# A decoder layer on one core: where the softmax work of its last stage runs

## Chip, cores and metric

One Trainium2 chip, one of its cores. The metric is the device time of one execution in microseconds (us). The arithmetic is float32; in the last stage the projections of the attention are done with float32 values split in two parts.

## What is computed

A layer on x of 32 sequences x 64 tokens x 512: a selective-scan block, a cross-attention to ctx_4096 (also 32 x 64 x 512) and a mixture of 64 rank-8 experts, each behind a layer norm and added to x. The change touches the cross-attention alone:

```python
q = (query @ Wq).reshape(nb, q_len, H, D).transpose(0, 2, 1, 3)      # H = 32 heads, D = 128
k = (key @ Wk).reshape(nb, q_len, KVH, D).transpose(0, 2, 1, 3)      # KVH = 8
v = (value @ Wv).reshape(nb, q_len, KVH, D).transpose(0, 2, 1, 3)
q = q * cos + _rotate_half(q) * sin
k = k * cos + _rotate_half(k) * sin
k = jnp.repeat(k, GROUPS, axis=1)                                    # GROUPS = 4
v = jnp.repeat(v, GROUPS, axis=1)
scores = jnp.einsum('bhqd,bhkd->bhqk', q, k) / jnp.sqrt(jnp.float32(D))
scores = jnp.where(mask == 0, jnp.float32(-1000000000.0), scores)
attn = jax.nn.softmax(scores, axis=-1)
x = jnp.einsum('bhqk,bhkd->bhqd', attn, v)
return x.transpose(0, 2, 1, 3).reshape(nb, q_len, H * D) @ Wo
```

## The kernel before

The 2048 tokens are four blocks of 512 (8 sequences each). Every engine runs one hand-written program, `one(i, mamba, attn, nxt)`, five times: stage 0 does the scan block of block 0, stages 1 to 3 the scan block of block i beside the attention of block i-1, and the last stage (`mamba` false) only the attention and the experts of the last block. The order on each engine is that of the text; semaphores (`stage` objects, one count per index) tie the engines together.

The attention goes by pairs of heads, o = 0 to 15, in steps: `step(jj, p, tail)` is step o = 2 jj + p. "Even" is p = 0, "odd" p = 1. In the last stage step o has these parts:

- TensorE (PE): `turn_probs` (L1647) transposes the probabilities of o, and waits for them (`prdy`) and for the low part of o-1 (`olo`); `project_o(o-1)` (L1675, 24 matmuls) waits for `olo`; `scores(o+1)` (L1636) waits for the rotated q (`qrdy`) and k (`krdy`); `values(o)` (L1662); `project_q(o+2)` (L1598, 24 matmuls) waits until the scores of o+1 are read (`srd`).
- VectorE (DVE): `mask_scores` (L1227) and `max_scores` (L1233) of o+1; in even steps `rope_k(jj+1)` (L1182, L1183, L1186 with kT and kr); `invert_sum` (L1237) and `probs` (L1241) of o+1; `o_low(o)` (L1287, two instructions: output minus its rounded high part); `rope_q(o+2)` (L1182, L1183, L1186 with qp and qr), which waits for the swapped q (`qrd`).
- ScalarE (ACT): `evac_pt(o)` (L879), `exps(o+1)` (L865: 8 instructions of 64 columns, each with its maximum as bias and its sum accumulated), `evac_o(o)` (L888), `swap_q(o+2)` (L839, L840).
- GpSimd (POOL): `split_wq(o+2)` and `split_wo(o+1)`: for each a TENSOR_SCALAR for the high part (L673) and a TENSOR_TENSOR for the low part (L675), of 128x1024 floats in SBUF. `split_wo(o+1)` waits for `project_o(o-1)` and is followed by the q split of the next step.
- SyncE (SP) loads the weights; before it loads the next k it waits for `krdy`, with later weight loads behind it.

Steps 0 to 12 that are even rotate a k, seven in all; steps 14 and 15 (`tail`) have no q to project, and step 15 no softmax. `rope_k` reads k1, kr, cosT and sinT, all in SBUF; `rope_q` reads PSUM and cosT (L1182), qr and sinT (L1183), qp and qr (L1186).

Of the kernel before, what the change touches and what calls it, by code (L numbers as in the profile page):

```python
# [25 lines left out]
P = 128  # L26
# [53 lines left out]
def build(nc, a, out):  # L80
    ctx = ExitStack()
    with ctx:
# [152 lines left out]
        def stage(name, per):  # L235
            return Stage(nc, ctx, name, per)
# [102 lines left out]
        wos = stage("wo_split", PAIRS)  # L339
        olo = stage("o_lo_ready", PAIRS)  # L340

        x2r = stage("x2_ready", TT)
# [462 lines left out]
        def _(eng):  # L805
# [26 lines left out]
            def one(i, mamba, attn, nxt):  # L832
# [28 lines left out]
                def exps(jj, o):  # L861

                    eng.wait_ge(smx.sem, smx.upto(blk, o) + jj * 2)
                    for b in range(NB):
                        ins = S.activation(pr[:, b, :], sc[:, b, :], ACT.Exp, bias=mx[:, b:b + 1],  # L865
                                           accum_out=sm[:, b:b + 1])
                    ins.then_inc(exd.sem, 1)
# [37 lines left out]
                def step(jj, p, tail):  # L905
# [6 lines left out]
                    if mamba:  # L912
                        decay(jj, p, 2)
                        decay(jj, p, 3)
                    if attn and not last:
                        exps(jj, p + 1)
                    if mamba and not last:
                        decay(jj, p + 1, 0)
                    if attn:
                        evac_o(jj, p)  # L920
# [157 lines left out]
        def _(eng):  # L1078
            lead(eng, ln1, ln1n, cv, ssv, ssi, sstr, spd, ur, inr, ch_n, ch_c, ch_f, scd, hcd, yad, pid, qt1, qt2, kt1, kt2, qrdy,
                 krdy, q1r, q2r, srd, smx, rcp, prdy, x2r, ln3, ln3n, rmd, zgd, outr, ch_p, ch_a, yr, x1r,  # L1080
                 ln2, ln2n, ch_m, olo)
            V = nc.vector
# [90 lines left out]
            def times_c(i, jj, p, c):  # L1173

                eng.wait_ge(scd.sem, scd.upto(i, NCH * p + c) + jj * (2 * NCH))
                h3 = hs[:, c, :].rearrange("p (d t) -> p d t", t=T)
                V.tensor_tensor(h3, h3, bc[:, p, 1:2, :].to_broadcast([P, 2, T]), ALU.mult).then_inc(hcd.sem, 1)  # L1177

            def attention_of(blk, mamba):
# [50 lines left out]
                def max_scores(jj, o):  # L1230

                    eng.wait_ge(srd.sem, srd.upto(blk, o) + jj * 2)
                    V.tensor_reduce(mx[:, :], sc[:, :, :], AX.X, ALU.max, negate=True).then_inc(smx.sem, 1)  # L1233

                def invert_sum(jj, o):
                    eng.wait_ge(exd.sem, exd.upto(blk, o) + jj * 2)
                    V.reciprocal(sm[:, :], sm[:, :]).then_inc(rcp.sem, 1)  # L1237
# [5 lines left out]

                return rope_q, rope_k, mask_scores, max_scores, invert_sum, probs

# [3 lines left out]
            def one(i, mamba, attn, nxt):  # L1249
                blk = i - 1  # L1250
                rope_q, rope_k, mask_scores, max_scores, invert_sum, probs = attention_of(blk, mamba)
                if not mamba:
# [14 lines left out]
                if attn:  # L1267
                    eng.wait_ge(s_mask, blk * 32 + 32)
                    eng.wait_ge(rop.sem, rop.upto(blk, 0))
                    rope_k(0)  # L1270
                    rope_q(0, 0)
                    for part in (mask_scores, max_scores, invert_sum, probs):
                        part(0, 0)
                    rope_q(0, 1)
# [17 lines left out]
                def step(jj, p, tail):  # L1292
# [15 lines left out]
                    if soft:  # L1308
                        max_scores(jj, p + 1)
                    if not mamba and not tail and p == 0:  # L1310
                        rope_k(jj + 1)
                    if mamba:
# [4 lines left out]
                    if mamba:  # L1317
                        times_c(i, jj, p, 2)
                    if soft:
                        invert_sum(jj, p + 1)  # L1320
                    if mamba:
                        times_c(i, jj, p, 3)
                    if soft and not mamba:
                        probs(jj, p + 1)
                    if not mamba:
                        o_low(jj, p)
                    if attn and not tail:
# [719 lines left out]
```

## Time and profile before

| | us |
|---|---|
| median of 3 runs | 2364.16 (2362.36 to 2365.87) |
| the profiled execution | 2367.41 |
| its span in the trace | 2365.6 |
| PE busy | 2095.8 (89%) |
| DVE busy | 1802.3 (76%) |
| ACT busy | 1058.3 (45%) |
| POOL busy | 588.8 (25%) |

The chain that ended last is, over the whole span, 41% DVE, 31% PE, 16% issue, 6% DMA and 4% ACT. The last stage is a small part of the span, so these shares say little of it; it is read by its own window, its own part of the chain and the timeline of its steps. In a timeline each line is a start, a duration, the engine, the line of the program, the operation with output and inputs, and in brackets how long the engine had been idle and what released it.

### The profile page before, as it was taken

Reading aid. Unit: us, or ns where it says so; the run is one execution under the profiler, and the core shown is the slowest. Engines: PE = TensorE matmul, PEld = TensorE weight load, DVE = VectorE, ACT = ScalarE, POOL = GpSimd, SP = SyncE. Lnnn points to the kernel's source line nnn. Section 1 sums busy time; section 2 is a strip of 40 time slices with the busy share of each in tenths; the row PEclk is TensorE's granted clock in tenths of the full one; section 3 lists DMA queues with packets and bytes.
Section 4 is the critical chain, followed back from the end, with each engine's and each line's share of the span. In section 5 each row is a group of like instructions: output and inputs, shape, how many; then the busy total and the mean of one; then the engine's idle time right before and its main releaser. Section 6 shows DMA issues by size and latency. Waiting matters only on the chain.

```text
span 2365.6 us, 27225 instructions
## 1 busy us (share of the span) xinstructions
PE 2095.8 (89%) x8272; PEld 1188.3 (50%) x8272; DVE 1802.3 (76%) x1816; ACT 1058.3 (45%) x2615; POOL 588.8 (25%) x408
## 2 busy tenths in 40 slices
PE   6877888989999979998999988998999979799988
PEld 2332453445555534445555543445555544477774
DVE  3499994389999985259999996359999995355653
ACT  2544441465555522266555542255655550243331
POOL 0089991001111111001111111001111111556650
PEclk9788999889999999989999999989999999899999
DMA  1468984238888881237888873236888874322310
GB/s 63 157 159 195 213 211 132 63 125 178 172 192 177 177 193 45 84 114 154 176 176 193 178 151 105 80 111 135 176 184 167 186 148 132 112 89 85 98 58 18
DMA packets 110121, 328.98 MB, mean 139 GB/s; under 512 B 12992, under 2 KB 13120, under 8 KB 107616
## 3 DMA queue, kind: packets, MB, share of 16 engines
q0 software_dynamic: 35328, 127.94, 29.1%
q1 hardware_dynamic: 68960, 189.58, 26.7%
q10 hardware_dynamic: 5760, 10.49, 1.2%
q8 instruction: 45, 0.74, 0.1%
q14 instruction: 28, 0.23, 0.0%
HBM read 183.00 MB, written 14.94 MB: 84 GB/s over the span
## 4 chain that ended last, share of the span: by engine, by line
DVE 41%; PE 31%; issue 16%; DMA 6%; ACT 4%; DVEq 1%; SPq 1%; POOL 1%; POOLq 0%; ACTq 0%; PEldq 0%
DVE hs L1170 13%; PE acc L1553 5%; DVE hs L1177 5%; DMA xc<-hs 4%; DVE hs L1342 4%; PE acc L1675 4%; DVE hs L1161 3%; PE pq L1606 2%; DVE qr L1207 2%; PE acc L1688 2%; PE acc L1767 2%; PE pq L1844 2%; PE pq L1636 2%; DVE sc L1227 2%; PE pk L1844 2%
## 5 line engine op out<-in xcount | busy, mean ns | idle before, releaser
L713 POOL DMA_DIRECT2D xc<-hs x192 | 165.8, 866 | 1305.9 <-DVE hs L1177 1269.0
L1170 DVE TENSOR_TENSOR_SCAN hs<-dA,hs 128x1024 f32<-128x1024 f32 x192 | 429.0, 2277 | 0.0
L900 ACT ACTIVATE dA<-dt,aneg 128x504 f32<-128x504 f32 x384 | 253.5, 707 | 253.6 <-DVE hs L1170 253.4
L1606 PE MATMUL pq<-qT,wa 128*128 128x512 f32 x768 | 353.8, 615 | 9.4 <-DVE sc L1227 9.4
L1688 PE MATMUL acc<-wb,oT 128*128 128x512 f32 x768 | 354.9, 607 | 3.6 <-ACT oT L888 3.6
L1177 DVE TENSOR_TENSOR hs<-hs,bc 128x1024 f32<-128x1024 f32 x256 | 308.2, 1206 | 2.2
L865 ACT ACTIVATE pr<-sc,mx 128x64 f32<-128x64 f32 x512 | 170.8, 335 | 243.1 <-DVE mx L1233 243.1
L1553 PE MATMUL acc<-xnT,wa 128*128 128x512 f32 x512 | 232.3, 607 | 12.4 <-PE acc L1553 4.7
L1606 PEld LDWEIGHTS pq<-qT,wa 128*128 128x128 f32 x768 | 146.6, 196 | 183.3 <-issue 173.1
L1161 DVE TENSOR_TENSOR hs<-u,bc 128x1024 f32<-128x1024 f32 x192 | 226.5, 1220 | 11.2 <-ACT xc L983 5.9
L1688 PEld LDWEIGHTS acc<-wb,oT 128*128 128x128 f32 x768 | 142.4, 195 | 149.7 <-issue 145.6
L1636 PE MATMUL pq<-kT,qp 128*128 128x64 f32 x1024 | 187.4, 285 | 23.8 <-DVE qp L1186 14.0
L1636 PEld LDWEIGHTS pq<-kT,qp 128*128 128x128 f32 x1024 | 158.0, 202 | 56.4 <-issue 40.6
L1553 PEld LDWEIGHTS acc<-xnT,wa 128*128 128x128 f32 x512 | 96.4, 193 | 146.5 <-issue 130.5
L1638 PE MATMUL pq<-k2T,qr 128*128 128x64 f32 x768 | 154.4, 284 | 0.0
L1227 DVE COPY_PREDICATED sc<-mask,pq 128x512 f32<-128x512 int32 x64 | 46.6, 729 | 104.2 <-PE pq L1636 58.6
L1638 PEld LDWEIGHTS pq<-k2T,qr 128*128 128x128 f32 x768 | 122.4, 201 | 0.0
L738 POOL TENSOR_TENSOR qp<-u,bc 128x1024 f32<-128x1024 f32 x32 | 92.9, 2904 | 107.9 <-ACT xc L983 107.7
L1647 PE MATMUL pk<-ident,pr 128*128 128x128 f32 x256 | 43.0, 294 | 83.8 <-ACT pr L873 62.0
L738 POOL TENSOR_TENSOR qr<-u,bc 128x1024 f32<-128x1024 f32 x32 | 100.5, 3141 | 7.2 <-DVE hs L1342 7.2
L1119 DVE SCALAR_TENSOR_TENSOR xc<-acc,cw,xc 128x504 f32<-128x504 f32 (+2 forms) x96 | 69.9, 734 | 42.1 <-ACT xc L823 39.6
L1620 PEld LDWEIGHTS pk<-wv,ctxT 128*128 128x128 f32 x768 | 87.7, 192 | 25.5 <-issue 24.5
(234 smaller groups left out, 3363.5 us busy)
## 6 DMA issues: line engine op xcount, KB each, us to landing
xc<-hs POOLq DMA_DIRECT2D x240, 512.0 KB, 7.0
bc<-bc_rows SPq DMA_DIRECT2D x64, 512.0 KB, 7.5
wa<-in_wq SPq DMA_DIRECT2D x64, 512.0 KB, 9.8
wb<-in_wo SPq DMA_DIRECT2D x64, 512.0 KB, 5.2
wa<-in_wx SPq DMA_DIRECT2D x16, 512.0 KB, 4.6
wa<-in_wz SPq DMA_DIRECT2D x16, 512.0 KB, 6.1
wb<-in_ow SPq DMA_DIRECT2D x16, 512.0 KB, 6.3
k<-k_rows SPq DMA_DIRECT2D x32, 256.0 KB, 11.1
```

What stands on the lines that cost most here:

```text
L713: G.dma_start(xc[:, 2 * c:2 * c + 2, :], hs[:, c, :].rearrange("p (d t) -> p d t", t=T), accum_op=ALU.add).then_inc(s_y[c], 16)
L738: G.tensor_tensor(inputs[c % 2].rearrange("p (d t) -> p d t", t=T), u[:, 2 * c:2 * c + 2, :], bc[:, p, 0:1, :].to_broadcast([P, 2, T]), AL ...
L865: ins = S.activation(pr[:, b, :], sc[:, b, :], ACT.Exp, bias=mx[:, b:b + 1], accum_out=sm[:, b:b + 1])
L900: ins = S.activation(to[:, :, 1:SEQ], dt[:, s, :].rearrange("p (b t) -> p b t", t=SEQ)[:, :, 1:SEQ], ACT.Exp, scale=aneg[:, s, bass.ds(jj ...
L1161: V.tensor_tensor(hs[:, c, :].rearrange("p (d t) -> p d t", t=T), u[:, 2 * c:2 * c + 2, :], bc[:, p, 0:1, :].to_broadcast([P, 2, T]), ALU. ...
L1170: V.tensor_tensor_scan(out=hs[:, c, :], data0=dA[:, c % 2, :], data1=hs[:, c, :], initial=0.0, op0=ALU.mult, op1=ALU.add).then_inc(scd.sem, 1)
L1177: V.tensor_tensor(h3, h3, bc[:, p, 1:2, :].to_broadcast([P, 2, T]), ALU.mult).then_inc(hcd.sem, 1)
L1553: ins = M.matmul(banks(s % 4), wa4((s // 2) % 2)[:, k, (s % 2) * P:(s % 2 + 1) * P], xnT[:, k, :], start=(k == 0), stop=(k == KE - 1))
L1606: ins = M.matmul(pq[:, h, :], wa4(p)[:, k, h * P:(h + 1) * P], qT[:, k, :], start=(k == 0), stop=(k == KE - 1))
L1636: ins = M.matmul(pq[:, 0, seq], qp[:, b, :], kT[:, seq], start=True, stop=not mamba)
L1638: ins = M.matmul(pq[:, 0, seq], q2[:, b, :], k2T[:, seq], start=False, stop=True)
L1688: ins = M.matmul(acc[:, t, :], oT[:, h, t * P:(t + 1) * P], wb2(o % 2)[:, h, :], start=False, stop=(stop and h == 1))
```

## The change

In the last stage only (`not mamba`):

- `max_scores` signals a semaphore of its own; a new `shift_scores` on VectorE adds the (negated) maxima to the scores, writing them to pr; one exponential on ScalarE works on all 512 columns of pr in place; a new `sum_probs` on VectorE adds up the probabilities, and `invert_sum` waits for it. The 8 exponentials with bias and accumulated sum are gone there.
- ScalarE evacuates the output (`evac_o`) ahead of the exponential of the next pair, not behind it.
- VectorE makes the low part of o between `shift_scores` and `sum_probs`, not behind `probs`.
- `rope_k(jj+1)` moves from behind `max_scores` to behind `probs`, ahead of `rope_q`.

```diff
--- before.py
+++ after.py
@@ -338,6 +338,8 @@
         woh = stage("wo_hi", PAIRS)
         wos = stage("wo_split", PAIRS)
         olo = stage("o_lo_ready", PAIRS)
+        lmx = stage("last_scores_max", PAIRS)
+        psm = stage("last_probs_summed", PAIRS)
 
         x2r = stage("x2_ready", TT)
         ln3 = stage("ln3_variance", 1)
@@ -861,6 +863,9 @@
                 def exps(jj, o):
 
                     eng.wait_ge(smx.sem, smx.upto(blk, o) + jj * 2)
+                    if not mamba:
+                        S.activation(pr[:, :, :], pr[:, :, :], ACT.Exp).then_inc(exd.sem, 1)
+                        return
                     for b in range(NB):
                         ins = S.activation(pr[:, b, :], sc[:, b, :], ACT.Exp, bias=mx[:, b:b + 1],
                                            accum_out=sm[:, b:b + 1])
@@ -912,11 +917,13 @@
                     if mamba:
                         decay(jj, p, 2)
                         decay(jj, p, 3)
+                    if not mamba:
+                        evac_o(jj, p)
                     if attn and not last:
                         exps(jj, p + 1)
                     if mamba and not last:
                         decay(jj, p + 1, 0)
-                    if attn:
+                    if mamba and attn:
                         evac_o(jj, p)
                     if mamba and not last:
                         decay(jj, p + 1, 1)
@@ -1078,7 +1085,7 @@
         def _(eng):
             lead(eng, ln1, ln1n, cv, ssv, ssi, sstr, spd, ur, inr, ch_n, ch_c, ch_f, scd, hcd, yad, pid, qt1, qt2, kt1, kt2, qrdy,
                  krdy, q1r, q2r, srd, smx, rcp, prdy, x2r, ln3, ln3n, rmd, zgd, outr, ch_p, ch_a, yr, x1r,
-                 ln2, ln2n, ch_m, olo)
+                 ln2, ln2n, ch_m, olo, lmx, psm)
             V = nc.vector
             eng.wait_ge(s_init, 3)
             eng.wait_ge(s_aneg, 1)
@@ -1230,10 +1237,25 @@
                 def max_scores(jj, o):
 
                     eng.wait_ge(srd.sem, srd.upto(blk, o) + jj * 2)
-                    V.tensor_reduce(mx[:, :], sc[:, :, :], AX.X, ALU.max, negate=True).then_inc(smx.sem, 1)
+                    V.tensor_reduce(mx[:, :], sc[:, :, :], AX.X, ALU.max, negate=True).then_inc(
+                        smx.sem if mamba else lmx.sem, 1)
+
+                def shift_scores(jj, o):
+
+                    eng.wait_ge(lmx.sem, lmx.upto(0, o) + jj * 2)
+                    V.tensor_tensor(pr[:, :, :], sc[:, :, :], mx[:, :].unsqueeze(2).to_broadcast([P, NB, SEQ]),
+                                    ALU.add).then_inc(smx.sem, 1)
+
+                def sum_probs(jj, o):
+
+                    eng.wait_ge(exd.sem, exd.upto(blk, o) + jj * 2)
+                    V.tensor_reduce(sm[:, :], pr[:, :, :], AX.X, ALU.add).then_inc(psm.sem, 1)
 
                 def invert_sum(jj, o):
-                    eng.wait_ge(exd.sem, exd.upto(blk, o) + jj * 2)
+                    if mamba:
+                        eng.wait_ge(exd.sem, exd.upto(blk, o) + jj * 2)
+                    else:
+                        eng.wait_ge(psm.sem, psm.upto(0, o) + jj * 2)
                     V.reciprocal(sm[:, :], sm[:, :]).then_inc(rcp.sem, 1)
 
                 def probs(jj, o):
@@ -1241,14 +1263,15 @@
                     V.tensor_tensor(pr[:, :, :], pr[:, :, :], sm[:, :].unsqueeze(2).to_broadcast([P, NB, SEQ]),
                                     ALU.mult).then_inc(prdy.sem, 1)
 
-                return rope_q, rope_k, mask_scores, max_scores, invert_sum, probs
+                return rope_q, rope_k, mask_scores, max_scores, shift_scores, sum_probs, invert_sum, probs
 
             norm_in(0)
             convolve(0)
 
             def one(i, mamba, attn, nxt):
                 blk = i - 1
-                rope_q, rope_k, mask_scores, max_scores, invert_sum, probs = attention_of(blk, mamba)
+                rope_q, rope_k, mask_scores, max_scores, shift_scores, sum_probs, invert_sum, probs = attention_of(
+                    blk, mamba)
                 if not mamba:
 
                     for k in range(KE):
@@ -1269,8 +1292,13 @@
                     eng.wait_ge(rop.sem, rop.upto(blk, 0))
                     rope_k(0)
                     rope_q(0, 0)
-                    for part in (mask_scores, max_scores, invert_sum, probs):
-                        part(0, 0)
+                    mask_scores(0, 0)
+                    max_scores(0, 0)
+                    if not mamba:
+                        shift_scores(0, 0)
+                        sum_probs(0, 0)
+                    invert_sum(0, 0)
+                    probs(0, 0)
                     rope_q(0, 1)
                 if mamba:
                     softplus(i, ch)
@@ -1307,8 +1335,6 @@
                         times_c(i, jj, p, 1)
                     if soft:
                         max_scores(jj, p + 1)
-                    if not mamba and not tail and p == 0:
-                        rope_k(jj + 1)
                     if mamba:
                         scan_input(i, jj, p, 2)
                         scan_input(i, jj, p, 3)
@@ -1316,14 +1342,20 @@
                         scan(i, jj, p, 3)
                     if mamba:
                         times_c(i, jj, p, 2)
+                    if soft and not mamba:
+                        shift_scores(jj, p + 1)
+                    if not mamba:
+                        o_low(jj, p)
+                    if soft and not mamba:
+                        sum_probs(jj, p + 1)
                     if soft:
                         invert_sum(jj, p + 1)
                     if mamba:
                         times_c(i, jj, p, 3)
                     if soft and not mamba:
                         probs(jj, p + 1)
-                    if not mamba:
-                        o_low(jj, p)
+                    if not mamba and not tail and p == 0:
+                        rope_k(jj + 1)
                     if attn and not tail:
                         rope_q(jj, p + 2)
                         if mamba and p == 0:
```

## Rows read from the trace of the kernel before

**Rows 1.** Windows of the last stage's steps: busy (instructions), granted clock, DMA share, GB/s.

```profile
2029.00:2303.70 274.70, 237.38 (x1302) 197.16 (x1301) 155.04 (x170) 103.55 (x340) 162.44 (x62) 0.93 0.28 91
```

**Rows 2.** The chain in order of time, last stage: start, us, engine and line.

```profile
2132.81 1.75 PE pq L1636 x16
...
2143.87 5.47 PE acc L1675 x24
2149.34 1.75 PE pq L1636 x16
...
2164.48 1.75 PE pq L1636 x16
...
2175.54 7.07 PE acc L1675 x24
...
2293.97 1.75 PE pq L1636 x16
```

**Rows 3.** Timeline, PE: the transposes of an even step, then of an odd one.

```profile
2143.24 0.63 PE L1647 MATMUL pk<-ident,pr 128*128 128x128 f32 x4 [1.93 <-DVE oT_lo L1287]
...
2158.39 0.63 PE L1647 MATMUL pk<-ident,pr 128*128 128x128 f32 x4 [0.57 <-DVE oT_lo L1287]
```

**Rows 4.** Timeline, DVE: even step 4.

```profile
2134.78 0.74 DVE L1227 COPY_PREDICATED sc<-mask,pq 128x512 f32<-128x512 int32 x1 [2.76 <-PE pq L1636]
2135.55 0.69 DVE L1233 TENSOR_REDUCE mx<-sc 128x8 f32<-128x512 f32 x1
2136.16 2.65 DVE L1182 TENSOR_TENSOR kT<-k,cosT 128x512 f32<-128x512 f32 x1
2138.73 1.52 DVE L1183 TENSOR_TENSOR kr<-kr,sinT 128x512 f32<-128x512 f32 x1
2140.36 0.69 DVE L1186 TENSOR_TENSOR kT<-kT,kr 128x512 f32<-128x512 f32 x1
...
2141.20 0.69 DVE L1241 TENSOR_TENSOR pr<-pr,sm 128x512 f32<-128x512 f32 x1
...
2143.50 1.22 DVE L1182 TENSOR_TENSOR qp<-pq,cosT 128x1024 f32<-128x1024 f32 x1 [0.41 <-ACT qr L840]
...
2145.96 1.23 DVE L1186 TENSOR_TENSOR qp<-qp,qr 128x1024 f32<-128x1024 f32 x1
```

**Rows 5.** Timeline, POOL: the same step.

```profile
2133.01 2.77 POOL L673 TENSOR_SCALAR wo_hi<-wb 128x1024 fp32r<-128x1024 f32 x1 [3.97 <-PE acc L1675]
2135.86 2.40 POOL L675 TENSOR_TENSOR wo_lo<-wb,wo_hi 128x1024 fp32r<-128x1024 f32 x1
2138.62 2.82 POOL L673 TENSOR_SCALAR wq_hi<-wa 128x1024 fp32r<-128x1024 f32 x1 [0.37 <-POOL wo_lo L675]
2141.52 2.59 POOL L675 TENSOR_TENSOR wq_lo<-wa,wq_hi 128x1024 fp32r<-128x1024 f32 x1
```

**Rows 6.** Timeline, DVE and POOL: the normalisation of odd step 5.

```profile
2155.78 1.26 DVE L1241 TENSOR_TENSOR pr<-pr,sm 128x512 f32<-128x512 f32 x1
...
2155.46 2.77 POOL L673 TENSOR_SCALAR wq_hi<-wa 128x1024 fp32r<-128x1024 f32 x1 [0.68 <-POOL wo_lo L675]
```

**Rows 7.** Timeline, ACT: the end of the swap in step 4.

```profile
2142.45 1.01 ACT L840 ACTIVATE qr<-pq 64x1024 f32<-64x1024 f32 x1
```

**Rows 8.** Groups by line and shape, ACT, whole span: an activation of 512 columns in SBUF.

```profile
L827 ACT ACTIVATE xc<-xc 128x512 f32<-128x512 f32 x32 | 19.9, 622 | 14.7 <-DVE xc L1119 14.6
```

**Rows 9.** Timeline, DVE and POOL: the first q rotation of the stage.

```profile
2042.75 1.87 DVE L1186 TENSOR_TENSOR qp<-qp,qr 128x1024 f32<-128x1024 f32 x1
...
2042.09 3.18 POOL L673 TENSOR_SCALAR wq_hi<-wa 128x1024 fp32r<-128x1024 f32 x1 [0.53 <-POOL wo_lo L675]
```

**Rows 10.** Window of a slow output projection, PE: busy, granted clock, DMA share, GB/s.

```profile
2175.50:2182.60 7.10, 7.10 (x27) 0.76 0.50 164
```

**Rows 11.** Timeline, POOL and PE: the tail's step 14.

```profile
2297.01 2.34 POOL L675 TENSOR_TENSOR wo_lo<-wb,wo_hi 128x1024 fp32r<-128x1024 f32 x1
...
2302.59 1.08 PE L1647 MATMUL pk<-ident,pr 128*128 128x128 f32 x4 [5.79 <-DVE oT_lo L1287]
```

## The prediction

> **What bounds the kernel now.** I read the windows by stage first. The steps of the last stage take 274.70 us, with TensorE busy for 237.38, VectorE for 155.04, ScalarE 103.55 and GpSimd 162.44 [rows 1]. TensorE is near its bound, and a change on other engines can give back at most its idle time. Next the chain in order of time: it repeats by pairs of steps. Call X the end of an output projection, where the next scores begin. From X of step 4 (2132.81) to that of step 5 (2149.34) it is 16.53, and from there to step 6 (2164.48) 15.14 [rows 2]. So an even step costs 1.4 more. The timeline of TensorE says where: ahead of the transposes of the probabilities it idles 1.93 in the even step and 0.57 in the odd one, each time until the low part of o is ready [rows 3]. That low part stands last in VectorE's queue. In the even step the rotation of k stands ahead of it, and there its first multiplication takes 2.65 and its second 1.52, where the subtraction of the same size takes 0.69 [rows 4].
>
> **Who stretches them.** Beside these rows I lay GpSimd's. The multiplication of 2.65 starts at 2136.16 and ends at 2138.81, and GpSimd's subtraction for the weight split runs from 2135.86 to 2138.26 [rows 4, 5]. If the multiplication really works for its usual 0.69, it began at 2138.12, which is 2.26 after GpSimd started. The second starts beside the next split's TENSOR_SCALAR (2138.62) and ends at 2140.25. So it began 0.9 to 1.0 after that, and 2140.36 runs at 0.69 inside the same TENSOR_SCALAR [rows 4, 5]. The normalisation of the odd step, 1.26 for 0.69, ends 1.58 after a TENSOR_SCALAR begins: again 0.9 of waiting [rows 6]. The other way round GpSimd takes 2.59, not 2.40, where the normalisation was running when it came [rows 4, 5]. The reduction at 2135.55 and the masking (one operand from PSUM) keep their usual times [rows 4]. From this I take two prices. A VectorE operation with two operands in SBUF waits until 2.26 behind the start of a GpSimd TENSOR_TENSOR, and 0.9 behind that of a TENSOR_SCALAR. Operations with one operand in SBUF wait for neither.
>
> The Trainium skill (SBUF — State Buffer, section "SBUF: two separate sides") calls this an exclusive lock of a shared port pair, which whichever starts first has "for the whole instruction". The trace agrees for the TENSOR_TENSOR. For the TENSOR_SCALAR it doesn't: the whole 2.8 would have pushed 2140.36 behind 2141.44.
>
> **The even step after, part by part**, in us from X of step 4, if GpSimd keeps its times (low parts at +3.05 and +8.71, high part of q at +5.81) [rows 5]:
> - Mask and maximum end at +3.43 [rows 4]. The added shift is due at +3.46. It reads scores and maxima, both in SBUF, as the normalisation reads its two, and falls into the GpSimd subtraction that stretched the k multiplication. Bounds: 0.69 (nothing holds it, end +4.15) and 2.5 (end +6.00, just where that multiplication ends). I take +6.00, for the slot and the operand places are the same.
> - One exponential for 16 instructions: 0.62 for 512 columns in SBUF is the nearest row [rows 8]; double is a safe upper bound. It starts at +6.04 and ends by +6.7, at worst +7.3. The low part of o (1.28 for both, one operand in PSUM) runs beside it to +7.21, as ScalarE now has o ready by about +4. So the exponential costs nothing; without that cover it would cost its 0.7.
> - The sum of the probabilities is as large as the maximum's reduction, 0.69: end +7.83. It holds up the reciprocal, the normalisation and both rotations behind it, and through them TensorE. Reciprocal (0.20) to +8.06, normalisation to +8.78, clear of the held stretches.
> - Transposes at +8.93, where they now start at 10.43 (2143.24) [rows 3]. TensorE itself is done with the q projection at +8.50 (2143.24 less its idle 1.93). The output projection ends 6.10 behind the transposes (2143.24 to 2149.34 [rows 2, 3]), at +15.03. By this alone the even step would gain 1.5.
> - The moved rotation of k now stands ahead of the rotation of q. It is due at +8.70, and GpSimd's next subtraction at +8.71. Whichever comes first, one of the two multiplications waits out that subtraction. If it is the first, they end at 10.97 + 0.69 + 0.61, and the k subtraction ends at +13.07; if it is the second, +12.95. Unheld it would be +10.8. The swapped q is there at 2143.46, +10.65 [rows 7], so the held rotation delays the q rotation by 2.3.
> - The q rotation takes 3.69 in all (2143.50 to 2147.19) [rows 4]. Its last part, a subtraction with both operands in SBUF, would be due at +15.34 to +15.46. But GpSimd's next split starts 0.20 behind X (2133.01) [rows 5], now at +15.23, and its TENSOR_SCALAR holds that subtraction for 0.9, as one was held in the first q rotation (1.87 for 1.23 [rows 9]). It ends at +17.35, and the scores start at +17.40, against 16.53. TensorE waits 2.37 there.
>
> So the even step loses 0.87 on balance: the gap ahead of the transposes moves to a larger one ahead of the scores.
>
> **The odd step after it.** Its scores start 2.37 late beside GpSimd, so the shift (due +3.46 from the scores) finds the subtraction over. Shift to +4.15, low part to +5.35, sum to +5.96, normalisation to about +6.9. TensorE is busy until about 8.5, so the gap of 0.57 is gone and the step takes 14.5: it gains 0.63.
>
> **SyncE.** The load of the next k waits for the rotated k, now some 5 us later, and two weight loads with it. Each of those tiles is split more than 15 us after it lands now, and the k is read a pair of steps later, so I put this at nothing; without that slack it would cost up to those 5 us a pair.
>
> **Sum.** Step 0: nothing, since its k rotation runs while TensorE is busy and GpSimd idle. Step 1: no late scores, normalisation ready 0.1 earlier, -0.1. Even steps 2 to 12: 6 x 0.87 = +5.2. Odd steps 3 to 11: 5 x -0.63 = -3.2. Step 13 -0.2 (no split beside it now). Step 14: transposes at 2302.59, 8.62 behind X (2293.97) [rows 2, 11]; with the shift held by the subtraction at 2297.01 [rows 11] at 8.93, +0.3. Together +2.0.
>
> Then TensorE's clock. In three of the six even-to-odd passages, each after the idle 1.93, the output projection takes about 7.07 for 5.47 [rows 2], at a granted clock of 0.76 in that stretch, a mix of 1.2 and 2.4 GHz [rows 10]: 1.6 each. After none of the gaps of 0.57 did it. The new gap is 2.37. Bounds: two drops of six (-1.6) and all six (+4.8). I take four, as the gap is longer and half of the shorter ones were followed by one: +1.6. Total +3.6: the profiled execution would go from 2367.41 to 2371.0, and the median from 2364.16 (3.3 below it) to 2367.8.
>
> **Rivals.**
> - *Clock*: five or six of the late scores are followed by a drop. It decides from the fifth on: +2.0 + 3.2 to 4.8, so +5.2 to +6.8, about 2371. For it: the gap grows by a fifth and comes every pair. Against: a drop followed only half of the old ones.
> - *The last q subtraction slips in ahead of GpSimd's split.* The margin is 0.1 to 0.2. Then the scores start at +16.7, the even step loses 0.14, and the sum is 0.8 - 3.2 - 0.1 - 0.2 + 0.3 = -2.4 with the drops unchanged: 2361.8.
> - *The shift isn't held* (the change does what its order suggests). Normalisation by +7.4, transposes at 8.5, k rotation unheld or held only in its last part, scores at +15.35: -1.2 x 6, -3.2 and -0.6 in the odd steps, -1.2 in step 14, and no gap long enough for a drop, -4.8: -17, 2347. Against it stands the k multiplication in the same slot.
> - *TENSOR_SCALAR holds for its whole time.* The last q subtraction would begin at 15.2 + 2.8 = 18.0 and the scores at 19.3: 6 x 2.7 - 3.2 = +13, 2377. This is what the rule of the Trainium skill cited above would give. The row at 2140.36 speaks against it.
>
> **How the numbers follow.** Forecast (three or four drops) 0.42, own range 2365.5 to 2369; clock rival 0.26; subtraction slips in 0.19; shift unheld 0.08; whole hold 0.05. The range 2357 to 2374 takes in the first three with their spread. A measurement of this kernel tells 0.2%, or 4.7 us, from no change. Faster by that: the unheld shift and the low tail of the third case, 0.16. Slower: clock rival, whole hold and a little of the forecast's own spread, 0.34. Within: 0.50.
>
> **What would show it.** In even steps: the shift at about 2.5 us, the first or second k multiplication at over 2, idle of about 2.4 ahead of the scores with the q subtraction as releaser, and transposes 8.9 behind X. In odd steps: a shift of 0.69 and almost no idle ahead of the transposes. A shift of 0.69 in even steps, or GpSimd's splits at other offsets, would make the prediction wrong.

## The result and the profile after

The kernel after the change takes 2377.9 us (median of 5 runs, 2366.15 to 2380.5), against 2364.16 before (median of 5, 2356.83 to 2365.87). The ratio is 1.0059, 95% interval 1.0036 to 1.0082: it is slower by 0.6%. That is 10.1 us above the forecast of 2367.8 and outside its range, which ended at 2374. The profiled execution of after took 2377.9 us itself, 10.5 more than that of before (2367.41).

First the page of after: its span, and the busy time of each engine.

```profile
span 2376.1 us, 27022 instructions
...
PE 2109.9 (89%) x8268; PEld 1199.6 (50%) x8272; DVE 1835.0 (77%) x1848; ACT 1025.9 (43%) x2375; POOL 591.8 (25%) x408
```

ScalarE lost 32.4 us of work and VectorE gained 32.7, and TensorE, whose work was not changed, is busy for 14.1 longer. So its own work runs slower somewhere. The same stretch as in [rows 1] (same columns: time, then busy time and instructions of TensorE, its weight loads, VectorE, ScalarE and GpSimd; granted clock, DMA share, GB/s), now of after:

```profile
2029.00:2303.70 274.70, 243.41 (x1263) 200.35 (x1264) 179.94 (x192) 67.02 (x93) 160.69 (x61) 0.91 0.27 87
```

The granted clock fell from 0.93 to 0.91 in it. Next the chain of waits of after in order of time (start, us, engine and line), which answers to [rows 2]. Each line of TensorE is the X of a step, here of steps 3 to 8:

```profile
2114.57 3.54 PE pq L1668 x16
...
2132.46 2.01 PE pq L1668 x16
...
2136.19 2.24 DVE pr L1246
...
2141.78 2.82 DVE kr L1190
...
2147.76 1.92 DVE qp L1193
...
2149.72 2.00 PE pq L1668 x16
...
2164.44 2.01 PE pq L1668 x16
...
2181.73 2.54 PE pq L1668 x16
...
2199.58 2.01 PE pq L1668 x16
```

From step 4 to 5 it is now 17.26 (2132.46 to 2149.72), for 16.53. From 5 to 6 it is 14.72, for 15.14. But from 3 to 4 and from 7 to 8, odd steps as well, it is 17.89 and 17.85. There the scores at the start take 3.54 and 2.54, not 2.00: the first run almost wholly at the low clock, the others in part. The timeline of TensorE (start, duration, engine, line, operation, count, and in brackets the idle time before and its releaser) shows the gap of the even step, the transposes that answer to [rows 3] and the scores behind them:

```profile
2141.23 0.66 PE L1679 MATMUL pk<-ident,pr 128*128 128x128 f32 x4
...
2149.72 2.00 PE L1668 MATMUL pq<-kT,qp 128*128 128x64 f32 x16 [2.36 <-DVE qp L1193]
```

The 1.93 ahead of the transposes are gone, and TensorE waits 2.36 ahead of the late scores instead, for the last subtraction of the q rotation. VectorE's timeline of the same step, to be laid beside [rows 4], and three lines of GpSimd's, beside [rows 5]:

```profile
2136.19 2.24 DVE L1246 TENSOR_TENSOR pr<-sc,mx 128x512 f32<-128x512 f32 x1
2138.34 1.27 DVE L1315 TENSOR_TENSOR oT_lo<-pk,oT_hi 128x512 fp32r<-128x512 f32 x2
2139.54 0.67 DVE L1252 TENSOR_REDUCE sm<-pr 128x8 f32<-128x512 f32 x1
2140.25 0.20 DVE L1259 RECIPROCAL sm<-sm 128x8 f32<-128x8 f32 x1
2140.48 0.69 DVE L1263 TENSOR_TENSOR pr<-pr,sm 128x512 f32<-128x512 f32 x1
2141.09 0.68 DVE L1189 TENSOR_TENSOR kT<-k,cosT 128x512 f32<-128x512 f32 x1
2141.69 2.89 DVE L1190 TENSOR_TENSOR kr<-kr,sinT 128x512 f32<-128x512 f32 x1
...
2147.76 1.91 DVE L1193 TENSOR_TENSOR qp<-qp,qr 128x1024 f32<-128x1024 f32 x1
...
2135.47 2.41 POOL L677 TENSOR_TENSOR wo_lo<-wb,wo_hi 128x1024 fp32r<-128x1024 f32 x1
...
2141.14 2.90 POOL L677 TENSOR_TENSOR wq_lo<-wa,wq_hi 128x1024 fp32r<-128x1024 f32 x1
...
2147.55 2.77 POOL L675 TENSOR_SCALAR wo_hi<-wb 128x1024 fp32r<-128x1024 f32 x1 [3.51 <-PE acc L1707]
```

Three operations with both operands in SBUF are held: the shift takes 2.24 beside GpSimd's first subtraction, the second k multiplication 2.89 beside its second, the q subtraction 1.91 beside the next TENSOR_SCALAR. All three stand where the forecast put them. What it missed is in the windows of TensorE behind two late scores (same columns as above; the first pair of numbers behind the time is TensorE's, the third number from the end is the granted clock), to be laid beside [rows 10]:

```profile
2114.60:2121.60 7.00, 7.00 (x36) 6.37 (x37) 2.41 (x4) 1.43 (x3) 6.15 (x4) 0.51 0.63 219
2149.70:2156.70 7.00, 6.98 (x49) 6.12 (x50) 4.66 (x8) 1.72 (x3) 6.24 (x3) 1.00 0.68 237
```

The gap ahead of both is the same. Behind the first the clock is at 1.2 GHz for nearly all of the 7 us (0.51), behind the second at 2.4. Cut into windows of half a microsecond, each of the four low stretches lasts 6.8 us; the three of before last 3.4. In [rows 10] a stretch as long was a mixture (0.76): about half of it low.

### The profile page after: what moved, and what is told of

Read it like the earlier page. It is cut to its first block, busy times and chain, and to the rows that moved or that the text cites. A ratio compares the mean times of both kernels' runs of the same rounds, so it can differ in the third digit from the quotient of the medians.

```text
span 2376.1 us, 27022 instructions
## 1 busy us (share of the span) xinstructions
PE 2109.9 (89%) x8268; PEld 1199.6 (50%) x8272; DVE 1835.0 (77%) x1848; ACT 1025.9 (43%) x2375; POOL 591.8 (25%) x408
## 4 chain that ended last, share of the span: by engine, by line
DVE 41%; PE 31%; issue 16%; DMA 7%; ACT 3%; DVEq 1%; SPq 1%; POOL 1%; POOLq 0%; ACTq 0%; PEldq 0%
DVE hs L1177 13%; DMA xc<-hs 6%; PE acc L1585 5%; DVE hs L1184 4%; DVE hs L1374 4%; DVE hs L1168 3%; PE pq L1630 3%; PE pq L1668 2%; PE pq L1638 2%; PE acc L1707 2%; DVE qr L1214 2%; PE acc L1720 2%; PE acc L1799 2%; PE pq L1876 2%; PE pk L1876 2%
## 5 line engine op out<-in xcount | busy, mean ns | idle before, releaser
L1668 PE MATMUL pq<-kT,qp 128*128 128x64 f32 x1024 | 192.6, 291 | 37.5 <-DVE qp L1193 28.1
L870 ACT ACTIVATE pr<-sc,mx 128x64 f32<-128x64 f32 x384 | 128.1, 334 | 110.1 <-DVE mx L1240 110.1
```

The source lines that it names most:

```text
L1668: ins = M.matmul(pq[:, 0, seq], qp[:, b, :], kT[:, seq], start=True, stop=not mamba)
```

## Experiments

Each kernel was compared with before on the same chip; the ratios are to before, with 95% intervals. "Passage" means the step from an even to an odd one, of which six matter (steps 2 to 12).

**Half of the change: the k rotation alone.** Before, with only `rope_k` moved.

```diff
                         max_scores(jj, p + 1)
-                    if not mamba and not tail and p == 0:
-                        rope_k(jj + 1)
...
                         o_low(jj, p)
+                    if not mamba and not tail and p == 0:
+                        rope_k(jj + 1)
```

> The kernel before with one edit: in the last stage the rotation of k moves from behind the maximum to just ahead of the rotation of q; softmax and low part as before. Theory (the moved rotation is held by GpSimd's subtraction and makes the scores late, and the late scores run at the low clock): transposes 9.06 behind X in even steps, scores at about +17.4 instead of +16.5, TensorE idle for over 2 us there, and after some four of six of these gaps a low clock for 6.8 us; in all about 10 us slower than before (2374, 2370 to 2378). Rival (the loss comes from the held shift and the sum on VectorE): within 3 us of before.

Measured: 2375.71, ratio 1.0044 [1.0021, 1.0067]. The move alone makes the gap (timeline of TensorE), and a mixed clock behind it (window, columns as above):

```profile
2147.85 2.16 PE L1636 MATMUL pq<-kT,qp 128*128 128x64 f32 x16 [2.36 <-DVE qp L1186]
...
2147.80:2154.80 7.00, 6.95 (x43) 6.10 (x44) 1.71 (x4) 3.12 (x17) 6.15 (x4) 0.76 0.66 223
```

The even step is 17.2 here, and the odd steps 3 to 11 are about 16.96 (2147.85 to 2164.81), 1.8 more than before's 15.15. All six passages have a low stretch, of 3.4 us in five of them and of 6.8 in the last. But in the five it isn't the clock that sets the pace. Before its transposes TensorE waits again (step 5, VectorE, GpSimd and TensorE):

```profile
2154.72 2.64 DVE L1241 TENSOR_TENSOR pr<-pr,sm 128x512 f32<-128x512 f32 x1
...
2154.41 2.39 POOL L675 TENSOR_TENSOR wq_lo<-wa,wq_hi 128x1024 fp32r<-128x1024 f32 x1
...
2158.70 0.63 PE L1647 MATMUL pk<-ident,pr 128*128 128x128 f32 x4 [0.58 <-DVE oT_lo L1287]
```

The eight exponentials end so late that the normalisation falls into GpSimd's low-part subtraction: it takes 2.64, where it took 1.26 in [rows 6]. The masking starts 2.34 behind X, for 1.91 before, and these 0.43 and the 1.38 of the hold are the 1.8. The low stretch runs in the shadow of that wait; of the 0.43 a few tenths at most are its own. (This is read from the rows; no run has this kernel without the low clock.) In step 13, where no q split stands beside it, there is no such hold, and there the low stretch of 6.8 us does cost time: the step is 17.86, for 14.69 before. So this half loses its time to GpSimd's hold twice, in even and in odd steps, and to the clock once: the 2374 that I expected came true for a partly different reason. It also shows that the same gap of 2.36 ahead of the same scores can bring a drop in six passages of six, and a short one in five.

**The other half: the softmax and the low part, k left in place.** After, with `rope_k` back behind `max_scores`, ahead of the shift.

```diff
                         max_scores(jj, p + 1)
+                    if not mamba and not tail and p == 0:
+                        rope_k(jj + 1)
...
-                    if not mamba and not tail and p == 0:
-                        rope_k(jj + 1)
```

> The changed kernel with the rotation of k back behind the maximum, ahead of the shift. Theory: the two operations with both operands in SBUF now stand one behind the other: k rotation done at +8.2, shift +8.9, normalisation held by the second subtraction to +11.7, transposes at +11.8 (before: 10.4); scores never late, the gap of about 3.3 is ahead of the transposes, and a low clock after it lasts 3.5. Even step 17.9, about 12 us slower than before (2376). Rival (all of the loss is the move of k): equal to before within 3 us, or faster.

Measured: 2376.93, ratio 1.0055 [1.0037, 1.0074]. The time is as expected, and the transposes come 11.67 behind X (expected 11.8). But the normalisation takes 0.71: I had expected it to be held, and GpSimd's subtraction had let go by the time it came. TensorE waits ahead of the transposes, for it:

```profile
2143.37 1.11 PE L1679 MATMUL pk<-ident,pr 128*128 128x128 f32 x4 [3.16 <-DVE pr L1263]
...
2142.80:2149.80 7.00, 6.43 (x24) 5.35 (x25) 4.10 (x4) 1.08 (x2) 0.00 (x0) 0.76 0.47 166
```

The even step is 19.3 with a drop in each, the odd one 14.95. Here the k rotation takes GpSimd's subtraction upon itself, and shift, low part and sum all stand behind it. So neither half is the culprit, and the two do not add: about +10 and +11 alone, +14 together. Each leaves TensorE a gap of over two microseconds per pair. And behind a gap of 3.16, longer than the 2.36 of after, the low stretch lasts only 3.4 us in all six even steps. Dense matmuls of 512 columns follow the gap here. That was a hint that the length of a gap alone doesn't set how long the clock stays low.

**Is it the clock? Zeros in the gap of after.** Eight matmuls of zeros into the accumulator (they change no value) are put where TensorE would idle. (`p` is 1 there: TensorE's text of odd step o comes behind the gap that VectorE's even step o-1 makes.)

```diff
                     if not last and late:
+                        if p == 1:
+                            for n in range(8):
+                                M.matmul(acc[:, n % TT, :], zeros[:, 0:P], zeros[:, :], start=False, stop=False)
                         scores(jj, p + 1)
```

> The changed kernel with 8 matmuls of zeros (128x512, bfloat16, added to the accumulators) ahead of the scores of each odd step of the last stage, where TensorE idles 2.36. Theory (the late scores cost 0.8 an even step by themselves and 3.2 more where they run at the low clock): the clock stays at 2.4 GHz in the passages, even steps stay at 17.3, odd steps are all 14.7, and the kernel is 10 to 13 us faster than the changed one, about 2366. Rival (the low clock has another cause than this idle time, or costs nothing): as the changed kernel, 2378.

Measured: 2365.45, ratio 0.9998 [0.9983, 1.0012], against 1.0059 for after. The scores begin as late as they did (even step 17.29), but no passage has a low clock any more:

```profile
2119.18 2.00 PE L1668 MATMUL pq<-kT,qp 128*128 128x64 f32 x16 [0.62 <-DVE qp L1193]
...
2119.10:2126.10 7.00, 6.92 (x49) 6.08 (x50) 4.62 (x9) 1.72 (x3) 6.24 (x3) 1.00 0.61 216
```

So the clock is worth some 12 us to this change, nearly all that it lost: four stretches of 3.15 are 12.6. That after now equals before doesn't mean that the new order costs nothing. From X of step 2 to X of step 14 it takes 191.96, for 194.46 in before, but 4.8 of before's are its own three low stretches. Without any, the new order is 2.3 slower: six even steps lose 0.75 each and five odd ones gain 0.43.

**The same for before.** Seven such matmuls ahead of the transposes, in the gap of the even step, where before idles for 1.93.

```diff
                     last = tail and p == 1
+                    if not mamba and p == 1:
+                        for n in range(7):
+                            M.matmul(acc[:, n % TT, :], zeros[:, 0:P], zeros[:, :], start=False, stop=False)
                     turn_probs(jj, p)
```

> The kernel before with 7 matmuls of zeros (128x512, bfloat16) ahead of the transposes of the odd steps of the last stage, where TensorE idles 1.93. Theory: no low clock in the passages; where the profile of before shows three of 1.6 us, this gives back about 5 us (2360). Rival (the low clock there costs nothing, since VectorE sets the pace): as before, within 1.5 us.

Measured: 2360.32, ratio 0.9988 [0.9978, 0.9998]: 2.7 us quicker, about half of what was expected. The trace has no low stretch in any passage, with steps of 16.56 and 15.15. So the clock cost before little. Beside this kernel, after with its gaps filled (2365.45) is the slower one by 5 us, though the intervals of the two ratios overlap. Of the gap in the first line of [rows 3] 0.41 are left.

**Does the length of the gap decide, or what follows it?** After, with the eight matmuls issued behind the wait for the late q, right ahead of the scores. The gap stays.

```diff
                         eng.wait_ge(krdy.sem, krdy.upto(blk, o // 2) + jj)
+                    if not mamba and not (isinstance(jj, int) and jj == 0 and o < 2) and o % 2 == 0:
+                        for n in range(8):
+                            M.matmul(acc[:, n % TT, :], zeros[:, 0:P], zeros[:, :], start=False, stop=False)
                     for b in range(NB):
```

> The changed kernel with 8 matmuls of zeros (128x512, bfloat16) behind the late wait of TensorE, right ahead of the scores of the odd steps: the idle time stays at 2.4, but what follows it is dense. Theory (a low clock lasts 6.8 us in the changed kernel and 3.4 before because scores and values of 64 columns follow the gap there): each low stretch in the passages lasts 3.4. The added work costs 1.7 to 3.4 us in each of the seven odd steps, less 1.6 to 1.7 for each of the four shorter low stretches: 5 to 12 us slower than the changed kernel (2383 to 2390). Rival (the length follows from the gap alone): low stretches still 6.8, over 15 us slower.

Measured: 2372.78, ratio 1.0036 [1.0022, 1.0050]. This is a miss. I expected half the length of low clock in most passages, and a kernel slower than after. Only one passage of six has a low stretch, and although the added work makes each odd step 1.6 longer, the median is 5 us lower than that of after (measured at another time, and the intervals of the two ratios overlap). TensorE's timeline (seven of the eight are recorded; with the first, of 0.22, the gap is 2.37, as in after), then the window behind that gap and the one with the low stretch:

```profile
2147.47 1.67 PE L1668 MATMUL acc<-zeros 128*128 128x512 bf16 x7 [2.59 <-DVE qp L1193]
...
2147.40:2154.40 7.00, 6.93 (x50) 5.59 (x50) 3.28 (x6) 1.72 (x3) 6.15 (x4) 1.00 0.63 214
2181.10:2188.10 7.00, 6.85 (x43) 4.79 (x43) 1.69 (x3) 0.80 (x2) 6.15 (x4) 0.77 0.51 185
```

The gap of after with dense matmuls behind it brought one drop in six, of 3.4 us; with scores and values of 64 and 128 columns behind it it brought four, of 6.8 us each. That speaks for a part of what follows. But the kernel with the k rotation alone has after's gap and after's scores behind it, and had six drops, five of them of 3.4 us. Taken together, all ten low stretches in passages where dense matmuls followed the gap (before three, k left in place six, this kernel one) lasted 3.4, and of the ten where light ones followed five lasted 6.8. The long ones stood only behind light work, but light work doesn't make them long each time, and what else decides is open. Nor does the length of the gap decide alone: 1.93 brought three drops of six in before, and 2.37 one of six here.

**Is it GpSimd's subtraction that decides the order?** After and before, both with GpSimd's low-part subtraction cut from 1024 to 64 columns, and the high part of the weights used in place of the low one. TensorE has as many matmuls as before, but the low part of the weights is left out of the result.

```diff
-                    G.tensor_tensor(two[1], raw, two[0].bitcast(F32), ALU.subtract).then_inc(both.sem, 1)
+                    few = slice(0, 64)
+                    G.tensor_tensor(two[1][:, few], raw[:, few], two[0][:, few].bitcast(F32), ALU.subtract).then_inc(both.sem, 1)
...
-                                    ins = M.matmul(pq[:, h, :], wq2[p][a_w][:, wcol], qT2[a_x][:, k, :],
+                                    ins = M.matmul(pq[:, h, :], wq2[p][0][:, wcol], qT2[a_x][:, k, :],
...
-                                                   wo2[o % 2][a_w][:, h * E:(h + 1) * E], start=False,
+                                                   wo2[o % 2][0][:, h * E:(h + 1) * E], start=False,
```

> The changed kernel, but in the last stage GpSimd subtracts only 64 of 1024 columns for the low parts of the weights, and TensorE reads the high part in place of the low one (as many matmuls; the low part of the weights is left out of the result). Theory (the second SBUF operand waits for GpSimd's subtraction and for nothing else): the shift takes 0.7 in even steps, k rotation 2.1 in all, scores on time, every step 14.5 to 14.8, no low clock in the passages; 15 to 18 us faster than the kernel before, about 2349. Rival (the added operations are too much for VectorE whoever holds them): even steps stay over 16.5.

> The kernel before with the same shortened subtraction and the high part in place of the low one. Theory: k rotation done at +6 instead of +8.2, transposes at about +8.6 in every step, no gap over 1 us, so every step 14.6 to 14.8: 13 to 16 us faster than before, about 2351, and within 3 us of the changed kernel with the same edit, which says that the order of the change is neither good nor bad without GpSimd's hold. Rival (the change's order is better by itself): this one slower than that one by over 4 us.

Measured: after 2344.23, ratio 0.9908 [0.9884, 0.9931]; before 2345.14, ratio 0.9921 [0.9897, 0.9945]. The two are equal now, within their intervals. An even step of after (step 4, X at 2125.17):

```profile
2128.21 0.32 POOL L678 TENSOR_TENSOR wo_lo<-wb,wo_hi 128x64 fp32r<-128x64 f32 x1
2128.89 2.78 POOL L675 TENSOR_SCALAR wq_hi<-wa 128x1024 fp32r<-128x1024 f32 x1 [0.37 <-POOL wo_lo L678]
2128.91 1.57 DVE L1247 TENSOR_TENSOR pr<-sc,mx 128x512 f32<-128x512 f32 x1
...
2133.75 0.69 DVE L1191 TENSOR_TENSOR kr<-kr,sinT 128x512 f32<-128x512 f32 x1
```

GpSimd's short subtraction is over when the shift comes, and the k multiplication that took 2.89 takes 0.69. The shift takes 1.57 and not the 0.7 that I expected: the next split's TENSOR_SCALAR now starts 0.02 ahead of it and holds it for the 0.9 of the forecast. That costs TensorE next to nothing: it is busy for 146.92 of the 147.16 us from step 4 to the end of step 13.

Every step takes 14.7 to 14.8 in both, even and odd, and of the gaps at most 0.2 is left. So GpSimd's low-part subtraction, and the operations that it holds, are the reason why the even step is long in both kernels, and without it the two orders cost the same. The gains are 18.8 and 17.9 us, where 15 to 18 and 13 to 16 were expected.

**What the forecast's reasoning points to: only the low part earlier.** In before, the row that TensorE waits for is the low part of o, last in VectorE's queue [rows 3]. It reads PSUM, so GpSimd does not hold it. This kernel takes from the change only that: `evac_o` ahead of the exponentials, and the low part ahead of the k rotation, in GpSimd's subtraction. Eight exponentials, k rotation and normalisation stay as they were.

```diff
+                    if not mamba:
+                        evac_o(jj, p)
                     if attn and not last:
                         exps(jj, p + 1)
...
-                    if attn:
+                    if mamba and attn:
                         evac_o(jj, p)
...
                         max_scores(jj, p + 1)
+                    if not mamba:
+                        o_low(jj, p)
                     if not mamba and not tail and p == 0:
                         rope_k(jj + 1)
...
-                    if not mamba:
-                        o_low(jj, p)
```

> The kernel before with one edit: in the last stage ScalarE evacuates o ahead of the exponentials and VectorE makes the low part of o right behind the maximum; exponentials with bias and sum, k rotation behind it, as before. Theory: low part done at +5.3, k rotation to +8.2 as before (the hold absorbs the 1.3), exponentials at +6.9, normalisation to +9.05, transposes at +9.2 in even steps (10.4 before) and without a gap in odd ones; rotation of q untouched, scores on time. Even step 15.3, odd step 14.6, no gap over 1 us and no low clock in the passages: 15 us faster than before, 2349. Rival (the k rotation is pushed back by the full 1.3): even step unchanged, 3 to 5 us faster.

Measured: 2346.72, ratio 0.9916 [0.9895, 0.9936]: 19 us quicker than before. VectorE's timeline of an even step, and TensorE's transposes:

```profile
2129.56 0.69 DVE L1235 TENSOR_REDUCE mx<-sc 128x8 f32<-128x512 f32 x1
2130.80 1.29 DVE L1289 TENSOR_TENSOR oT_lo<-pk,oT_hi 128x512 fp32r<-128x512 f32 x2 [0.56 <-ACT oT_hi L888]
2132.01 0.68 DVE L1184 TENSOR_TENSOR kT<-k,cosT 128x512 f32<-128x512 f32 x1
2132.61 1.52 DVE L1185 TENSOR_TENSOR kr<-kr,sinT 128x512 f32<-128x512 f32 x1
...
2135.83 0.66 PE L1649 MATMUL pk<-ident,pr 128*128 128x128 f32 x4 [0.51 <-DVE pr L1243]
```

The k multiplication that took 2.65 in [rows 4] takes 0.68, because the low part fills the time in which it would be held. The even step falls to 15.41 and the odd one to 14.43 (scores at 2126.55, 2141.96 and 2156.39), the largest gap in a passage to 0.52, and no passage has a low clock. The expectation had 15.3 and 14.6.

**And with the remaining gaps filled.** On top of it, 27 and 30 matmuls of zeros ahead of the first two scores, into accumulators not yet in use, and 20 ahead of the last transposes.

```diff
+                    if not mamba and last:
+                        for n in range(20):
+                            M.matmul(acc[:, n % TT, :], zeros[:, 0:P], zeros[:, :], start=False, stop=False)
                     turn_probs(jj, p)
...
                     if not last and late:
+                        if first:
+                            for n in range(30):
+                                M.matmul(acc[:, n % TT, :], zeros[:, 0:P], zeros[:, :], start=True, stop=True)
                         scores(jj, p + 1)
...
+                    if not mamba:
+                        for n in range(27):
+                            M.matmul(acc[:, n % TT, :], zeros[:, 0:P], zeros[:, :], start=True, stop=True)
                     scores(0, 0)
```

> The kernel with only the early low part, and matmuls of zeros (128x512, bfloat16) where TensorE still idles in the last stage: 27 ahead of the first scores, 30 ahead of the second (both 7 us idle, then 13.6 us at the low clock), 20 ahead of the last transposes. Theory (what follows these gaps is slow only for the clock, so the low clock is worth its matmuls): first and second scores 1.75 instead of 3.68 each, the two q projections behind them 1.7 shorter each, about 6 to 8 us less at the start and 1 to 3 at the end: 2338 (2334 to 2342). Rival (that stretch is paced by VectorE): within 3 us of the kernel without the filling, 2347.

Measured: 2338.95, ratio 0.9896 [0.9876, 0.9916], the lowest median of all: 25 us below before on its chip, where the kernel without the filling was 19 below (the intervals of the two ratios overlap a little). The expectation was 2338. The first scores, which took 3.69 at the low clock in before (the chain's line at 2044.67), now run at the high one:

```profile
2043.17 2.00 PE L1638 MATMUL pq<-kT,qp 128*128 128x64 f32 x16 [0.71 <-DVE qp L1188]
```

## Why the prediction was wrong

I go by its own terms, for the profiled executions, which differ by 10.5 us (2367.41 to 2377.9); X is the start of the scores in the chain.

| term | predicted | measured | from |
|---|---|---|---|
| up to X of step 2 | -0.1 | -2.2 | 2099.51 to 2097.27 |
| six even steps | +5.2 | +4.5 | 17.28 less 16.53, each |
| odd steps 3 to 13, clock apart | -3.4 | -2.2 | 14.72 less 15.15, five of them; step 13: 0 |
| clock in the passages | +1.6 | +7.8 | 4 x 3.15 less 3 x 1.6 |
| behind X of step 14 | +0.3 | +2.6 | 71.6 to 74.2, to the end of the span |
| sum | +3.6 | +10.5 | |

**The mechanism of the even step: right.** The shift was held (2.24; forecast 2.5), the k rotation was held in its second multiplication (2.89), the q subtraction by the next split (1.91 for 1.23), TensorE idled 2.36 (forecast 2.37) with that subtraction as releaser, and the transposes came 8.77 behind X (forecast 8.93). The step takes 17.28 where 17.40 were forecast. The equal times of the two kernels with a short subtraction show that the holds by GpSimd's subtraction separate the two orders. The same prices carried the kernel with only the low part moved.

The Trainium skill (SBUF — State Buffer, section "SBUF: two separate sides") lets whichever of the two engines starts first keep the shared port pair for its whole instruction. The trace agrees for GpSimd's TENSOR_TENSOR. For its TENSOR_SCALAR it again does not: the q subtraction came 0.21 behind the TENSOR_SCALAR of 2147.55 and ended at 2149.67, 0.65 before that did.

**The odd step: right in kind.** The shift takes 0.69 there and the gap of 0.57 is gone, but the step is 14.72, not 14.5: a third of the gain did not come. Step 13 gained nothing.

**The failed step: the price of a clock drop.** The forecast said, "I take four", and four of six passages had one. That count was a choice between two and six, and that it came true was luck: the kernel with the k rotation alone, with the same gap, had six. The forecast then priced each drop at 1.6, read from [rows 2] and [rows 10]. There the gap stood ahead of 24 matmuls of 512 columns, and 3.4 of the 7.1 us were at the low clock. The change moved the gap ahead of scores and values of 64 and 128 columns, and behind it the clock stayed low for 6.8 us: an odd step costs 17.87 instead of 14.72, so 3.15. Four drops at twice the price are 6.2 us more than forecast. The kernel with zeros in the gap shows that the clock is the cause of the loss (ratio 0.9998 for 1.0059). Why the clock stayed low for twice as long isn't shown; the work behind the gap may have a part in it, but the k rotation alone has the same work there and stretches of 3.4. I had seen the gap move and had re-counted its drops by its length, but I had taken the price of one from another place in the program.

**The end: chance, by the same engine.** The transposes of step 14 come 8.73 behind X, for 8.62 before, so the change in work cost 0.1. The other 2.5 come behind them, where the work is the same in both kernels. In the 34 us from there the granted clock is 0.91 before and 0.82 after (windows of both, before first):

```profile
2303.00:2337.00 34.00, 29.50 (x130) 19.19 (x129) 13.89 (x43) 5.50 (x12) 2.94 (x4) 0.91 0.00 0
```

```profile
2311.00:2345.00 34.00, 29.84 (x115) 19.58 (x113) 12.44 (x34) 4.32 (x9) 2.94 (x4) 0.82 0.00 0
```

The forecast had no term for it. The other traces show that it isn't the change that brings it. From these transposes to the end it is 63.0 us in before and 65.5 in after. But it is 63.1 in after with its gaps filled (0.90 in those 34 us) and 65.5 in before with the k rotation moved, whose code there is that of before. One low stretch more comes in some executions and not in others.

**Up to step 2.** 2.1 of the 2.2 us are there at the first scores of the stage (2044.67 and 2042.59), ahead of which the code is the same. In the other kernels' traces in which it is unchanged as well these scores start between 2040.39 and 2046.17, so this is scatter between executions. **From the profiled execution to the median.** Before, the median lay 3.3 below the profiled execution, and I took that off for after as well. After's profiled execution was its median, and the 3.3 were lost there: with the 7 of the sum they make up the miss of 10.1.

**The rivals.** The clock rival (five or six drops at 1.6) had the right cause and the wrong form; its 2371 was still too low. None of the others came true: the q subtraction did not slip in ahead of the split, the shift was held, and the whole hold fell. That whole hold would have given 2377, near the time measured, but the rows refute it, which shows that a total alone proves no mechanism.

## What to carry to other kernels

Give a stretch in which GpSimd holds the SBUF operands of VectorE to work that reads PSUM, and only then move the rest: one such move was worth 19 us here, and reordering around it cost 14. When a wait of the bound engine moves, price it anew where it lands, even if the wait is hardly longer: what a drop cost ahead of dense matmuls was half of what it cost ahead of small ones here. Where TensorE idles for two microseconds, a few matmuls of zeros in the gap are a cheap test of how much of a loss is the clock. And a low clock costs little while another engine's wait covers it, as in the odd steps of the kernel with the k rotation alone: look for the wait behind it before you price it.

## What the runs showed of the hardware

- The low clock (1.2 GHz) didn't follow the length of a gap, which I had not expected. Gap 1.93, then transposes and dense matmuls: three passages of six, 3.4 us each. Gap 3.16, then the same: six of six, 3.4 us. Gap 2.37, then eight dense matmuls of 512 columns: one of six, 3.4 us. Gap 2.36, then matmuls of 64 and 128 columns: four of six in after, 6.8 us each; six of six in the kernel with the k rotation alone, five of 3.4 us and one of 6.8. The Trainium skill (TensorE: Matmul & The Clock Gate, "Part 1: The HAM clock gate") has the rate follow "how busy the PE has been recently" and these runs agree as far as they go: matmuls of zeros in the gap kept it at 2.4 GHz.
- A GpSimd TENSOR_TENSOR on 128x1024 floats holds a VectorE operation with two SBUF operands for nearly all of its 2.4 us. The shift came 0.72 behind its start and ended at 2138.43, 2.26 + 0.69 behind it: the price that was read from the trace of before.
- One exponential of 128x512 in place took 0.63 us in the last stage, as the row of 0.62 had suggested:

```profile
L867 ACT ACTIVATE pr<-pr 128x512 f32<-128x512 f32 x16 | 10.1, 632 | 25.7 <-DVE pr L1246 25.7
```
